# A DLRM tower on one core: 13 instead of 7 embedding tables looked up by one-hot matmuls, Gram matmuls behind the last gather

## The chip, the cores and the metric

The kernel runs on 1 core of a Trainium2 chip. The core has five engines with queues of their own: PE (matmul), DVE (VectorE), ACT (ScalarE), POOL (GpSimd) and SP (SyncE, which here only issues transfers), and 16 DMA engines that they share. The metric is device microseconds per execution; the lower the better. The traces come from separate, profiled executions.

## The reference

A batch of 512 rows. Each row has a dense vector of 128 numbers and 26 ids, one for each embedding table. One table has 125,000 rows, nine have 12,500, eight have 1,250 and eight have 1,000; a table row is 128 fp32 numbers.

```python
e = jnp.stack([tbl_0[ids[:, 0]], ..., tbl_25[ids[:, 25]]], axis=1)       # 512 x 26 x 128
combined = jnp.concatenate([dense_features[:, None, :], e], axis=1)      # 512 x 27 x 128
interactions = jnp.einsum('bnd,bmd->bnm', combined, combined)            # 27 x 27 Gram matrix of each row
z = jnp.concatenate([dense_features, interactions[:, TRIU_I, TRIU_J]], axis=1)
h = jnp.concatenate([z, dense_features], axis=1)                         # 128 + 351 + 128 columns
h = jnp.maximum(h @ W_top1 + b_top1, 0.0)                                # 512
h = jnp.maximum(h @ W_top2 + b_top2, 0.0)                                # 256
y = h @ W_top3                                                           # 1
```

## The kernel before

The batch is worked in four **tiles** of 128 rows. A feature vector gets to the place where the Gram matmuls read it, `vecs_t` (number d on partition d, then tile, row, slot), in one of two ways.

**Gathered tables** (the 19 largest). POOL issues one indirect transfer for each tile and table (L273), 76 in all, in order of tiles; each brings 128 table rows to `vecs`, which has room for two tiles. PE turns them by transposes, four slots at a time (`turn`, L329, groups of slots in `GROUPS`, five to a tile with the dense vector in slot 0), into one of two PSUM tiles `turned`, and DVE copies them to `vecs_t` (`copy_slots`, L422). POOL may write a group of tile t + 2 once the turn of the same group of tile t is done.

**Looked-up tables** (seven with 1,000 rows). SP loads the whole table (L231, L234) and the ids, repeated on all partitions (L236). The table lies in 7 blocks of 128 rows and one of 104. ACT rounds it to `table_hi` (L478), DVE forms the rest, `table_lo` (`split_table`, L414). For each block a one-hot matrix, table row by batch row, is made from the ids: six by DVE in one comparison each (`make_one_hot`, L407), two by ACT in two operations each (L491, L497). PE multiplies each block's high and low part with it (`look_up`, L347), all 512 batch rows at once, summing in PSUM, and ACT copies the sum to `vecs_t` (L502).

**Gram and layers**, for each tile. `products` (L366) issues 128 matmuls of 29 x 27, one for each batch row; in the trace each is two records. DVE and ACT copy the blocks to `prods` (`copy_products`, L210 and L215), each half of them. `mlp1` (L285, L287) is the first layer, in four quarters, `mlp2` (L309) the second and `mlp3` (L316) the third; ACT applies bias and relu (L461, L470), and DVE copies the result out of PSUM (L390). The sum of a lookup lies in the PSUM tiles of the Gram, so the first Gram also waits for the last lookup's copy.

Each engine works through its own list in order: `TENSOR_STEPS`, `VECTOR_STEPS`, `SCALAR_STEPS`. A wait at the head of an engine's queue holds all behind it. Before, PE's list puts tile 0's turns between the lookups and then, tile by tile, a Gram, with the next tile's turns and this tile's layers between Grams. SP issues the loads in order and holds a table's load until a buffer of raw table is free.

## Time and profile before

| | us |
|---|---|
| median of 3 timed runs | 135.42 |
| lowest, highest | 133.78, 136.95 |
| span of the profiled execution | 176.1 |
| PE busy, 1520 matmul records | 101.0 |
| DVE busy | 67.0 |
| ACT busy | 61.3 |
| POOL busy, 76 of 84 instructions are gathers | 79.1 |
| mean granted clock of TensorE, share of full speed | 0.806 |

For the profiled execution no other time than its span is given. The page says for how long each engine was busy, in 40 slices, and who released whom; an idle time put down to "issue" is one in which the engine waited for nothing that the profile shows. PEld is the loading of weights, which runs beside PE. Times within an execution count from its first instruction. Matmul records overlap, so the step from one start to the next is the pace, not the duration of one. A gather's record ends when its descriptors are written; its bytes move after that.

### The profile page before, as it was taken

The page shows a single profiled execution, that of the slowest core. Times are in us where ns is not written, and L with a number is a line of the kernel's source. Part 1 is how long each engine was busy: PE and PEld are TensorE (multiplying, and loading weights), DVE is VectorE, ACT ScalarE, POOL GpSimd, SP SyncE. Part 2 cuts the span into 40 slices and gives each one's busy share as a digit, 9 for nine tenths or more (in the row PEclk, how much of TensorE's full clock was granted, in tenths as well). Part 3 has the DMA queues.
Part 4 walks back from the last instruction along what each step waited for, and adds up shares of the span by engine and source line. Part 5 has one row for each costly group of instructions (what it writes and reads, how often), then busy time and mean ns, then how long its engine had stood idle before and what let it go on. Part 6 is the DMA issues. An engine that isn't in the chain of part 4 may idle for free.

```text
span 176.1 us, 3483 instructions
## 1 busy us (share of the span) xinstructions
PE 101.0 (57%) x1520; PEld 87.4 (50%) x1520; DVE 67.0 (38%) x117; ACT 61.3 (35%) x115; POOL 79.1 (45%) x84
## 2 busy tenths in 40 slices
PE   0059977529993211100005579378894989663983
PEld 0048756428872001000005479277893989553972
DVE  3588899524514000000000762008652793246000
ACT  2695997450841000000000820029411760247021
POOL 4777787777777777777720477600000000000000
PEclk9999997987998555555555678858999699998799
DMA  5986666992121212111210021200000000000000
GB/s 132 294 284 212 217 203 190 327 368 79 48 60 45 60 45 60 45 60 45 60 30 4 19 60 45 63 4 0 4 0 4 4 0 4 4 4 0 4 0 0
DMA packets 6773, 13.57 MB, mean 77 GB/s; under 512 B 2253, under 2 KB 3493, under 8 KB 6630
## 3 DMA queue, kind: packets, MB, share of 16 engines
q1 hardware_dynamic: 4325, 8.36, 14.9%
q0 software_dynamic: 2432, 4.99, 9.3%
q8 instruction: 12, 0.20, 0.5%
q14 instruction: 4, 0.02, 0.1%
HBM read 13.34 MB, written 0.00 MB: 76 GB/s over the span
## 4 chain that ended last, share of the span: by engine, by line
PE 36%; issue 31%; POOL 12%; DVE 12%; DMA 6%; ACT 2%; ACTq 0%; DVEq 0%
PE h_ps L287 14%; POOL vecs L273 12%; PE gram L366 10%; DVE prods L210 9%; PE gram L347 5%; DMA vecs<-tbl,idx 5%; PE h_ps L285 3%; PE turned L329 3%; DVE prods L215 1%; ACT vecs_t L502 1%; DVE vecs_t L422 1%; DMA idx<-ids 1%; PE h_ps L309 1%; ACT h L461 1%; PE h_ps L316 0%
## 5 line engine op out<-in xcount | busy, mean ns | idle before, releaser
L273 POOL DMA_INDIRECT vecs<-tbl,idx x76 | 78.2, 1029 | 33.6 <-issue 22.6
L366 PE MATMUL gram<-vecs_t 128*29 128x27 f32 x1024 | 18.0, 209 | 45.6 <-issue 43.9
L210 DVE COPY prods<-gram 29x192 f32<-29x192 f32 x32 | 15.7, 492 | 65.3 <-PE gram L366 64.4
L366 PEld LDWEIGHTS gram<-vecs_t 128*29 128x29 f32 x1024 | 14.6, 125 | 49.5 <-issue 47.4
L210 ACT COPY prods<-gram 29x192 f32<-29x192 f32 x32 | 15.8, 495 | 56.4 <-PE gram L366 55.7
L422 DVE COPY vecs_t<-turned 128x512 f32<-128x512 f32 x20 | 21.3, 1098 | 17.7 <-PE turned L329 14.2
L287 PE MATMUL h_ps<-prods,w_sb 128*128 128x128 f32 x192 | 26.5, 292 | 0.0
L287 PEld LDWEIGHTS h_ps<-prods,w_sb 128*128 128x128 f32 x192 | 25.1, 208 | 0.1
L347 PE MATMUL gram<-one_hot,table_hi 128*128 128x512 f32 (+1 forms) x56 | 25.1, 447 | 0.0
L347 PE MATMUL gram<-one_hot,table_lo 128*128 128x512 f32 (+1 forms) x56 | 24.3, 435 | 0.0
L407 DVE TENSOR_SCALAR one_hot<-ids_all,row_of 128x512 fp32r<-128x512 int32 x42 | 17.3, 482 | 5.5 <-PE gram L347 5.5
L329 PE MATMUL turned<-ident,vecs 128*128 128x128 f32 x76 | 14.5, 331 | 7.5 <-DMA vecs<-tbl,idx 7.0
L329 PEld LDWEIGHTS turned<-ident,vecs 128*128 128x128 f32 x76 | 11.5, 174 | 9.3 <-DMA vecs<-tbl,idx 7.9
L461 ACT ACTIVATE h<-h_ps,small_sb 128x128 f32<-128x128 f32 x16 | 4.6, 369 | 31.0 <-PE h_ps L287 17.4
L347 PEld LDWEIGHTS gram<-one_hot,table_hi 128*128 128x128 f32 (+1 forms) x56 | 12.3, 219 | 2.7
L347 PEld LDWEIGHTS gram<-one_hot,table_lo 128*128 128x128 f32 (+1 forms) x56 | 12.2, 217 | 2.7
L502 ACT COPY vecs_t<-gram 128x512 f32<-128x512 f32 x7 | 7.9, 1130 | 13.5 <-PE gram L347 11.0
L285 PE MATMUL h_ps<-dense_t,w_dense 128*128 128x128 f32 x32 | 7.2, 310 | 7.8 <-DVE prods L215 4.7
L414 DVE TENSOR_TENSOR table_lo<-table,table_hi 128x1024 fp32r<-128x1024 f32 x7 | 8.6, 1225 | 5.0 <-ACT table_hi L478 4.3
L285 PEld LDWEIGHTS h_ps<-dense_t,w_dense 128*128 128x128 f32 x32 | 5.5, 214 | 8.8 <-DVE prods L215 5.3
L491 ACT ACTIVATE distance<-ids_all,row_of 128x512 f32<-128x512 int32 x14 | 9.3, 710 | 0.5 <-DMA ids_all<-ids_t 0.5
L497 ACT ACTIVATE one_hot<-distance,one 128x512 fp32r<-128x512 f32 x14 | 9.2, 708 | 0.0
(26 smaller groups left out, 47.4 us busy)
## 6 DMA issues: line engine op xcount, KB each, us to landing
table<-tbl SPq DMA_DIRECT2D x7, 448.0 KB
w_sb<-w SPq DMA_DIRECT2D x1, 2048.0 KB
ids_all<-ids_t SPq DMA_DIRECT2D x7, 256.0 KB, 5.1
vecs<-tbl,idx POOLq DMA_INDIRECT x76
w_sb<-w SPq DMA_DIRECT2D x1, 512.0 KB
table<-tbl SPq DMA_DIRECT2D x7, 52.0 KB
dense_rows<-dense SPq DMA_DIRECT2D x1, 256.0 KB, 5.2
idx<-ids SPq DMA_DIRECT2D x1, 52.0 KB, 2.1
```

The lines of the kernel that those rows point to most:

```text
L210: copy(prods[QUAD * k:QUAD * k + ROWS, t % 2, :, q::QUADS], src[0:ROWS, :, FIRST_SLOT[k]:FIRST_SLOT[k] + CHUNKS] .rearrange("p b c -> p c ...
L273: nc.gpsimd.indirect_dma_start(out=vecs[:, t % 2, s, :], out_offset=None, in_=tables[f], in_offset=bass.IndirectOffsetOnAxis(ap=idx[:, t, ...
L285: nc.tensor.matmul(h1_ps[:, o, :], w_dense[:, cols], dense_t[:, t, :], start=True, stop=False)
L287: mm = nc.tensor.matmul(h1_ps[:, o, :], w1_sb[:, 2 + c, cols], prods[:, t % 2, c, :], start=False, stop=(c == CHUNKS - 1))
L329: mm = nc.tensor.transpose(turned[k % 2][:, j, :], vecs[:, t % 2, s, :] if s else dense_rows[:, t, :], ident[:])
L347: mm = nc.tensor.matmul(looked_up[j % 2], part[0:rows, j % PARTS, c, :], one_hot[0:rows, j % 2, c, :], start=(c == 0 and part is table_hi) ...
L366: mm = nc.tensor.matmul(gram[t % 2][QUAD * q:QUAD * q + ROWS, blk, 0:N], x[:, 0:ROWS], x[:, 0:N], start=True, stop=True)
L407: nc.vector.tensor_scalar(one_hot[:, j % 2, c, :], ids_all[:, j, :], at, None, ALU.is_equal).then_inc(hot_ok, 1)
L422: nc.vector.tensor_copy(vecs_t[:, t, :, slots[0]:slots[-1] + 1].rearrange("d r s -> d s r"), turned[k % 2][:, 0:len(slots), :]).then_inc(s ...
L491: nc.scalar.activation(distance[:, i, :], ids_all[:, j, :], ACT.Square, bias=at, scale=-1.0).then_inc(distance_ok, 1)
L497: nc.scalar.activation(one_hot[:, j % 2, c, :], distance[:, i, :], ACT.Relu, bias=one[:], scale=-1.0).then_inc(hot_scalar, 1)
L502: nc.scalar.copy(vecs_t[:, :, :, TURNED + j], looked_up[j % 2].rearrange("p (t r) -> p t r", t=TILES)).then_inc(look_out, 1)
```

## The change

Thirteen tables are looked up (all eight with 1,000 rows, five with 1,250) and 13 gathered, in 52 transfers. A looked-up table now lies on 125 partitions in 8 or 10 equal blocks (`TP`, `NBLK`), 114 in all, loaded in two parts of 112 and 13 partitions. DVE makes all one-hot blocks, into a ring of 16 (`HOT`) whose places come free one by one; ACT makes none, and does the slot copies of the first 13 turns in DVE's place. A lookup does all its high matmuls, then all its low ones; it has four places for its sums instead of two, and there are three buffers for raw tables. The ids come in three loads, and the weights behind table 7. The layouts of ids and dense vectors in memory are changed so that each partition reads one piece.

In the step lists, a lookup and a turn alternate 13 times, then come the other three turns (there are sixteen now, four to a tile), and then the four Grams with the layers between them.

```diff
-LOOKED_UP = 7
+LOOKED_UP = 13
+TP = 125
+SPREAD = 112
...
+NBLK = [TABLE_ROWS[f] // TP for f in LOOKUPS]
...
+RAW = 3
+PARTS = 2
+HOT = 16
+SUMS = 4
...
-TENSOR_STEPS = (
-    FIRST_STEPS + [("products", 0, 0)] + turns(1, EARLY, EARLY + 2) + first_layer(0)[:1]
-    + turns(1, EARLY + 2, NG) + first_layer(0)[1:]
...
+KEEP = 2
+IDS_PARTS = [(0, 1), (1, 4), (4, LOOKED_UP)]
+WEIGHTS_AFTER = 7
+LOOK_TURNS = [(step, n) for n in range(LOOKED_UP) for step in ("look", "turn")]
+TENSOR_STEPS = LOOK_TURNS + [("turn", n) for n in range(LOOKED_UP, len(TURNS))] + [
+    ("products", 0), ("products", 1),
+    ("layer1", 0), ("products", 2), ("layer2", 0), ("layer1", 1), ("layer3", 0), ("products", 3), ("layer2", 1),
+    ("layer1", 2), ("layer3", 1), ("layer2", 2), ("layer1", 3), ("layer3", 2), ("layer2", 3), ("layer3", 3),
+]
+VECTOR_STEPS = [("weights", 0)] + [("turn", n) for n in range(LOOKED_UP, len(TURNS))] + [
+    ("products", 0), ("products", 1), ("products", 2), ("layer3", 0), ("products", 3), ("layer3", 1),
+    ("layer3", 2), ("layer3", 3),
 ]
...
+            load_ids(0)
+            sp.dma_start(dense_rows[:], dense).then_inc(dense_in, 16)
+            load_table(sp, 1)
+            load_ids(1)
+            load_table(sp, 2)
+            load_ids(2)
+            for j in range(3, LOOKED_UP):
+                load_table(sp, j)
+                if j == WEIGHTS_AFTER:
+                    sp.dma_start(w1_sb[:], w1).then_inc(w_in, 16)
...
             def look_up(j):
-                if j >= 2:
-                    pe.wait_ge(look_out, j - 1)
+                if j >= SUMS:
+                    pe.wait_ge(look_out, j - SUMS + 1)
+                pe.wait_ge(hi_ok, j + 1)
+                for c in range(NBLK[j]):
+                    k = FIRST_HOT[j] + c
+                    pe.wait_ge(hot_ok, k + 1)
+                    nc.tensor.matmul(looked_up[j % SUMS], table_hi[0:TP, j % PARTS, c, :], one_hot[0:TP, k % HOT, :],
+                                     start=(c == 0), stop=False)
                 pe.wait_ge(lo_ok, j + 1)
...
-                mm.then_inc(look_ok, 1)
+                for c in range(NBLK[j]):
+                    k = FIRST_HOT[j] + c
+                    nc.tensor.matmul(looked_up[j % SUMS], table_lo[0:TP, j % PARTS, c, :], one_hot[0:TP, k % HOT, :],
+                                     start=False, stop=(c == NBLK[j] - 1)).then_inc(hot_used, 1)
             def products(t):
-                pe.wait_ge(slots_out, NG * (t + 1))
+                turn_is_out(pe, min(NG * (t + 1), LOOKED_UP) - 1)
+                turn_is_out(pe, NG * (t + 1) - 1)
                 pe.wait_ge(extra_out, 2 * (t + 1))
                 if t == 0:
                     pe.wait_ge(look_out, LOOKED_UP)
...
+            def make_one_hot(j):
+                if j == 0:
+                    dve.wait_ge(rows_ok, len(SIZES))
+                for i, (a, b) in enumerate(IDS_PARTS):
+                    if j == a:
+                        dve.wait_ge(ids_in[i], 16)
+                for c in range(NBLK[j]):
+                    k = FIRST_HOT[j] + c
+                    if k >= HOT:
+                        dve.wait_ge(hot_used, k - HOT + 1)
+                    at = row_of[0:TP, SIZES.index(NBLK[j]), c:c + 1]
+                    nc.vector.tensor_scalar(one_hot[0:TP, k % HOT, :], ids_all[0:TP, j, :], at, None,
+                                            ALU.is_equal).then_inc(hot_ok, 1)
...
+            for j in range(LOOKED_UP):
+                make_one_hot(j)
                 split_table(j)
...
+            load_table(act, 0)
+            for j in range(PARTS):
                 table_hi_part(j)
...
-                if j + 2 < LOOKED_UP:
-                    make_one_hot_blocks(j + 2)
-                if j + 3 < LOOKED_UP:
-                    table_hi_part(j + 3)
+                if j + PARTS < LOOKED_UP:
+                    table_hi_part(j + PARTS)
+                copy_slots(act, nc.scalar.copy, slots_act, j)
+                if j % NG == 0:
+                    extra_copies(j // NG)
```

PE's queue, before, behind the last lookup (`turned` is a turn, `gram<-vecs_t` a Gram, `h_ps` a layer; `gathered1_2` is tile 1's group 2):

```order
L329 MATMUL turned<-ident,dense_rows 128x128 [waits slots_out,gathered1_0]
L329 MATMUL turned<-ident,vecs 128x128 x3
L329 MATMUL turned<-ident,vecs 128x128 [waits slots_out,gathered1_1]
L329 MATMUL turned<-ident,vecs 128x128 x3
L366 MATMUL gram<-vecs_t 29x27 [waits look_out,extra_out,slots_out]
L366 MATMUL gram<-vecs_t 29x27 x127
L329 MATMUL turned<-ident,vecs 128x128 [waits slots_out,gathered1_2]
L329 MATMUL turned<-ident,vecs 128x128 x3
L329 MATMUL turned<-ident,vecs 128x128 [waits slots_out,gathered1_3]
L329 MATMUL turned<-ident,vecs 128x128 x3
L285 MATMUL h_ps<-dense_t,w_dense 128x128 [waits w_in,w_dense_ok,prods_act,prods_dve]
```

PE's queue, changed, from turn 13 (tile 3's group 1) on:

```order
L311 MATMUL turned<-ident,vecs 128x128 [waits slots_act,gathered3_1]
L311 MATMUL turned<-ident,vecs 128x128 x3
L311 MATMUL turned<-ident,vecs 128x128 [waits slots_act,gathered3_2]
L311 MATMUL turned<-ident,vecs 128x128 x3
L311 MATMUL turned<-ident,vecs 128x128 [waits slots_dve,gathered3_3]
L311 MATMUL turned<-ident,vecs 128x128
L344 MATMUL gram<-vecs_t 29x27 [waits extra_out,look_out,slots_act]
L344 MATMUL gram<-vecs_t 29x27 x127
L344 MATMUL gram<-vecs_t 29x27 [waits extra_out,slots_act]
L344 MATMUL gram<-vecs_t 29x27 x127
L279 MATMUL h_ps<-dense_t,w_dense 128x128 [waits w_in,w_dense_ok,prods_act,prods_dve]
```

Tile 0's Gram stood behind tile 1's second turn, and each further Gram behind its own tile's turns; now all four stand behind the last turn of tile 3. The turns of tiles 1 to 3 that lay between Grams and layers lie between lookups.

DVE's queue, before, for the first two looked-up tables (`table_lo` is a split, `vecs_t<-turned` the copy of a turn):

```order
L414 TENSOR_TENSOR table_lo<-table,table_hi 128x1024 [waits hi_ok]
L407 TENSOR_SCALAR one_hot<-ids_all,row_of 128x512 [waits ids_all_in0,rows_ok]
L407 TENSOR_SCALAR one_hot<-ids_all,row_of 128x512 x5
L414 TENSOR_TENSOR table_lo<-table,table_hi 128x1024 [waits hi_ok]
L407 TENSOR_SCALAR one_hot<-ids_all,row_of 128x512 [waits ids_all_in1]
L407 TENSOR_SCALAR one_hot<-ids_all,row_of 128x512 x5
L422 COPY vecs_t<-turned 128x4x128 [waits turned_ok]
L414 TENSOR_TENSOR table_lo<-table,table_hi 128x1024 [waits hi_ok]
```

DVE's queue, changed, for the first tables (split and one-hots of tables 0, 1, 2 and on):

```order
L382 TENSOR_SCALAR one_hot<-ids_all,row_of 125x512 [waits ids_in0,rows_ok]
L382 TENSOR_SCALAR one_hot<-ids_all,row_of 125x512 x7
L389 TENSOR_TENSOR table_lo<-table,table_hi 125x1024 [waits hi_ok]
L382 TENSOR_SCALAR one_hot<-ids_all,row_of 125x512 [waits ids_in1]
L382 TENSOR_SCALAR one_hot<-ids_all,row_of 125x512 x7
L389 TENSOR_TENSOR table_lo<-table,table_hi 125x1024 [waits hi_ok]
L382 TENSOR_SCALAR one_hot<-ids_all,row_of 125x512 [waits hot_used] x8
L389 TENSOR_TENSOR table_lo<-table,table_hi 125x1024 [waits hot_used,hi_ok]
```

The turn's copy is gone from between the tables, one-hots go ahead of their table's split, eight of them where there were six, and from the third table on each waits for a place in the ring (`hot_used`).

## Rows read from the trace of the kernel before

**Rows 1.** Waits: engine, line, what was waited for: total us, times, longest us.

```profile
PE gram L366 <- issue: 43.9, 33, 2.6
```

**Rows 2.** Timeline (start us, us, engine, what, [idle before]), PE, tile 0's Gram matmuls.

```profile
52.93 0.45 PE L366 MATMUL gram<-vecs_t 128*29 128x27 f32 x34 [0.39 <-ACT vecs_t L502]
...
87.83 0.20 PE L366 MATMUL gram<-vecs_t 128*29 128x27 f32 x1 [2.60 <-issue]
...
94.82 2.61 PE L366 MATMUL gram<-vecs_t 128*29 128x27 f32 x187 [0.50 <-issue]
```

**Rows 3.** Stretches: length, busy us (records) of PE, PEld, DVE, ACT, POOL; clock; DMA.

```profile
52.90:97.50 44.60, 8.71 (x257) 6.42 (x258) 1.80 (x3) 0.84 (x3) 27.54 (x29) 0.53 0.15 45
...
111.20:119.10 7.90, 4.28 (x257) 3.70 (x258) 0.01 (x1) 1.15 (x5) 1.89 (x2) 0.65 0.11 29
...
137.60:156.50 18.90, 15.28 (x353) 14.44 (x353) 10.00 (x16) 7.23 (x18) 0.00 (x0) 0.91 0.01 3
```

**Rows 4.** Timeline of PE, the Gram matmuls of tiles 2 and 3.

```profile
133.00 1.55 PE L366 MATMUL gram<-vecs_t 128*29 128x27 f32 x161 [0.64 <-DVE vecs_t L422]
...
136.57 1.00 PE L366 MATMUL gram<-vecs_t 128*29 128x27 f32 x95 [2.03 <-issue]
...
151.57 1.78 PE L366 MATMUL gram<-vecs_t 128*29 128x27 f32 x189 [0.64 <-DVE vecs_t L422]
...
155.73 0.77 PE L366 MATMUL gram<-vecs_t 128*29 128x27 f32 x67 [2.38 <-issue]
```

**Rows 5.** DMA queues of the whole span: packets, MB, share of 16 engines.

```profile
q8 instruction: 12, 0.20, 0.5%
```

**Rows 6.** Timeline of POOL, gathers 1, 19, 40, 64 and 76.

```profile
3.12 1.10 POOL L273 DMA_INDIRECT vecs<-tbl,idx  x1 [1.46 <-DMA idx<-ids]
...
29.81 0.94 POOL L273 DMA_INDIRECT vecs<-tbl,idx  x1 [0.30 <-issue]
...
58.31 0.94 POOL L273 DMA_INDIRECT vecs<-tbl,idx  x1 [0.30 <-issue]
...
88.27 0.94 POOL L273 DMA_INDIRECT vecs<-tbl,idx  x1 [0.30 <-issue]
...
112.48 0.94 POOL L273 DMA_INDIRECT vecs<-tbl,idx  x1 [0.30 <-issue]
```

**Rows 7.** DMA view, 112 to 115 us: bytes moved in 40 slices of 0.075 us.

```profile
GB/s 0 219 0 0 0 0 0 0 0 0 0 218 164 273 164 55 0 0 0 0 0 0 0 0 0 0 0 0 328 218 219 109 0 0 0 0 0 0 0 0
```

**Rows 8.** Timeline of DVE, one looked-up table: its split and six one-hot blocks.

```profile
21.35 1.23 DVE L414 TENSOR_TENSOR table_lo<-table,table_hi 128x1024 fp32r<-128x1024 f32 x1 [0.72 <-issue]
...
22.49 2.46 DVE L407 TENSOR_SCALAR one_hot<-ids_all,row_of 128x512 fp32r<-128x512 int32 x6
```

**Rows 9.** Timeline of PE, lookup matmuls after a wait and in the last stretch.

```profile
30.39 0.63 PE L347 MATMUL gram<-one_hot,table_hi 128*128 128x512 f32 x1
...
30.82 0.63 PE L347 MATMUL gram<-one_hot,table_lo 128*128 128x512 f32 x1
...
48.28 0.40 PE L347 MATMUL gram<-one_hot,table_hi 128*128 128x512 f32 x1
...
48.52 0.39 PE L347 MATMUL gram<-one_hot,table_lo 128*128 128x512 f32 x1
```

**Rows 10.** Timeline of PE, first-layer quarter, turn behind it, tile 3's last turn.

```profile
129.67 0.39 PE L285 MATMUL h_ps<-dense_t,w_dense 128*128 128x128 f32 x2
...
131.24 0.60 PE L329 MATMUL turned<-ident,vecs 128*128 128x128 f32 x4
...
149.80 0.60 PE L329 MATMUL turned<-ident,vecs 128*128 128x128 f32 x4
```

**Rows 11.** Timeline of DVE, half of the copies of tile 2's Gram blocks.

```profile
137.62 2.08 DVE L210 COPY prods<-gram 29x192 f32<-29x192 f32 x4 [4.57 <-PE gram L366]
...
139.73 0.33 DVE L215 COPY prods<-gram 27x96 f32<-27x96 f32 x1
```

**Rows 12.** Timeline of PE, what follows the last first layer.

```profile
169.45 0.60 PE L316 MATMUL h_ps<-h,small_sb 128*1 128x128 f32 x4
```

More of the change, by code:

```diff
@@ L51 @@
 TURNED = 1 + len(GATHERED)
-FULL = [TABLE_ROWS[f] // P for f in LOOKUPS]
-LAST = [TABLE_ROWS[f] % P for f in LOOKUPS]
-MAX_BLOCKS = max(FULL) + 1
-PARTS = 3
-BY_SCALAR = 2
-SIZES = sorted(set(FULL))
+NBLK = [TABLE_ROWS[f] // TP for f in LOOKUPS]
+MAX_BLOCKS = max(NBLK)
+SIZES = sorted(set(NBLK))
+RAW = 3
+PARTS = 2
+HOT = 16
+SUMS = 4
+FIRST_HOT = [sum(NBLK[:j]) for j in range(LOOKED_UP)]
+assert all(TABLE_ROWS[f] % TP == 0 for f in LOOKUPS)
 PER_GROUP = 4
@@ L62 @@
 NG = len(GROUPS)
+TURNS = [(t, g) for t in range(TILES) for g in range(NG)]
 QUARTERS = H1 // P
-def turns(t, first, end):
-    return [("turn", t, g) for g in range(first, end)]
-def first_layer(t):
-    return [("layer1", t, q) for q in range(QUARTERS)]
-EARLY = 2
-FIRST_TURNS = turns(0, 0, NG) + turns(1, 0, EARLY)
-FIRST_LOOKS = [("look", j, 0) for j in range(LOOKED_UP)]
-FIRST_STEPS = [x for pair in zip(FIRST_TURNS[:NG], FIRST_LOOKS) for x in pair]
-FIRST_STEPS += FIRST_LOOKS[NG:] + FIRST_TURNS[NG:]
@@ L120, in product_rows, with dlrm_tower @@
     return where
-def dlrm_tower(nc, dense, ids, ids_t, tables, w1, w2, small, out):
+def dlrm_tower(nc, dense, idx_rows, ids_look, tables, w1, w2, small, out):
     with ExitStack() as ctx:
@@ L177, in dlrm_tower @@
         hot_ok = sem("hot_ok")
[L178 removed]
+        hot_used = sem("hot_used")
         look_out = sem("look_out")
[L180 removed]
+        gathered = [[sem(f"gathered{t}_{g}") for g in range(NG)] for t in range(TILES)]
         ident_zero = sem("ident_zero")
@@ L199, in dlrm_tower, with looked, turn_is_out, load_table @@
         BY_ENGINE = 2 * (QUADS + 1)
+        def looked(j):
+            return FIRST_HOT[j] + NBLK[j]
+        def turn_is_out(engine, n):
+            if n < LOOKED_UP:
+                engine.wait_ge(slots_act, n + 1)
+            else:
+                engine.wait_ge(slots_dve, n + 1 - LOOKED_UP)
+        def load_table(engine, j):
+            f = LOOKUPS[j]
+            rows = tables[f].rearrange("(p c) d -> p c d", p=TP)
+            if j >= RAW:
+                engine.wait_ge(lo_ok, j - RAW + 1)
+            for a, b in [(0, SPREAD), (SPREAD, TP)]:
+                engine.dma_start(table[a:b, j % RAW, 0:NBLK[j], :], rows[a:b]).then_inc(table_in[j % RAW], 16)
+        def copy_slots(engine, copy, done, n):
+            t, g = TURNS[n]
+            engine.wait_ge(turned_ok, n + 1)
+            slots = GROUPS[g]
+            copy(vecs_t[:, t, :, slots[0]:slots[-1] + 1].rearrange("d r s -> d s r"),
+                 turned[n % 2][:, 0:len(slots), :]).then_inc(done, 1)
         def copy_products(engine, copy, done, t, quads):
@@ L568 @@
     out = nc.dram_tensor("y", (B, 1), F32, kind="ExternalOutput").ap()
-    dlrm_tower(nc, dense, ids, ids_t, tables, w1, w2, small, out)
+    dlrm_tower(nc, dense, idx_rows, ids_look, tables, w1, w2, small, out)
     r = run_bass_kernel_spmd(nc, [arrays], core_ids=[0])
```

269 lines of the change are left out of this document (87 added, 182 removed).

## The prediction

> **What bounds the kernel now.** I read the spans first: the profiled execution spans 176.1 us, the timed runs 133.8 to 137.0 us. A trace 40 us longer than the runs must hold time that they do not have, so the next view was the waits: PE's Gram matmuls (L366) stand idle 43.9 us in 33 gaps with nothing that releases them [rows 1]. The timeline puts nearly all in tile 0's Gram: from 52.9 to 94.8 us single matmuls lie up to 2.6 us apart while POOL issues gathers, and once POOL stops, 187 records follow in 2.6 us [rows 2, 6]. I read these gaps as the profile's own. As a stretch, tile 0's Gram took 44.6 us and tile 1's 7.9 [rows 3]; tiles 2 and 3, with no gathers beside them, took 133.00 to 137.57 and 151.57 to 156.50, 4.7 us on average, with one gap of 2.0 to 2.4 us in each [rows 4]. With 4.7 in place of 44.6 and 7.9 the span is 176.1 - 39.9 - 3.2 = **133.0 us**. The median run, 135.4, is 2.4 above; that I take as what lies around the span, and put on again at the end.
>
> In those 133 us: until 52.9 PE alternates turns and lookups; then it goes through four tiles, about 19 us each (137.6 to 156.5 [rows 3]), and gathers for tiles 2 and 3 arrive under that work. POOL's stream would then end at 88.27 + 12 x 1.248 = 103.2 at the last issue, 105.1 with the transfer, just ahead of tile 3's last turn (149.8 - 43.1 = 106.7 [rows 10]). So the kernel is bound by PE with its copies, and the gathers are hidden, barely.
>
> **The change, part by part.**
>
> *Gathers.* 52 instead of 76. Quiet, one follows another every (88.27 - 58.31) / 24 = 1.248 us. In the first 19, while DVE makes one-hots and splits, it is (29.81 - 3.12) / 18 = 1.483 [rows 6]. DVE's five sets of such work in that stretch are 5 x 3.6 = 18.0 us of 26.7, 67% [rows 8]. The change keeps DVE at it without turn copies, some 97%: the extra 0.235 us grows to 0.34, a pitch of 1.59.
>
> *Lookups on DVE.* One block takes 2.46 / 6 = 0.41 us, a split of 8 blocks 1.14 [rows 8], one of 10 by size 1.43. Eight tables of 8 blocks at 4.42 and five of 10 at 5.53 give 63.0 us (ScalarE makes no blocks now). From about 6 us, when ids and the first table are in, DVE ends at 69.
>
> *Lookups on PE.* 228 matmuls at 0.23 us at the high clock, 52 us; after a wait they go at 0.43 [rows 9]. Per table 3.7 (4.6) and a turn of 0.6: under DVE's 4.42 (5.53), hence hidden, if the clock holds. It then trails DVE by one table's low half: lookups end near 72 to 76.
>
> *Last gather.* By 69 us POOL is 41.4 pitches on; the other 9.6 go at 1.248: issue at 69 + 12.0 = 81.0, done 0.94 later, transfer 1.0 later (gather 76 ended at 113.42, its bytes moved until 114.4 [rows 6, 7]). **T0 = 83 us.** The bounds: at 1.248 throughout the last gather lands at 68.7 and the lookups with three turns decide, 74.5; at the worst of the lookups (below) 90.
>
> *What waits for T0.* The step list puts turns 13, 14 and 15 ahead of Gram 0; turn 15 waits for the last gather, and everything behind it on PE's queue with it: all four Grams and all twelve layer steps. DVE's queue holds the three turn copies ahead of its product copies, ScalarE's queue waits on Gram 0. Nothing of tiles 0 to 2 runs under the gathers any more.
>
> *The tail from T0.* A turn of four tables to the next Gram took 131.24 to 133.00, 1.76 [rows 4, 10]; two tables, 1.2. Four Grams at 4.7: 18.8. A first layer is four quarters of 1.57 (129.67 to 131.24) [rows 10], 6.3, times four 25.2. A second layer has 16 records where a quarter has 14: 1.8, three times 5.4 (the fourth is in the end). Two third layers 1.0. From the last first layer to the end 176.1 - 169.45 = 6.65 [rows 12]. The product copies take 2 x 2.45 = 4.9 us [rows 11]: Gram 1 hides tile 0's but for 0.2, later ones lie under the first layers. Second layer 2 waits for its relus, 1.3. The clock will be low after the waits for the last gathers: the mean of the stretch with the 187 records is 0.53, mostly the 1.2 GHz level [rows 3], and they took 13.9 ns each where tile 2's 161 took 9.6 [rows 2, 4]; for the first Gram and what follows it, 1.3. Sum 1.2 + 18.8 + 25.2 + 5.4 + 1.0 + 6.65 + 1.5 + 1.3 = **61.1 us**. By 83 + 61 = 144.1 the change costs 11.1 us on 133.0, for 24 gathers fewer.
>
> *Loads.* Tables and ids bring 7.3 + 3.4 MB in place of 3.5 + 1.8; the weights go out behind table 7. I cost this at nothing: DVE is two blocks of work ahead through the ring of 16, and T0 is some 7 us behind the lookups. If that cover goes, it is the second rival.
>
> *The single gap in each Gram.* Rows show one gap of 2.03 and 2.38 us in tiles 2 and 3 after 161 and 189 records, with 95 + 96 + 189 = 380 matmul records between them (257 of the 353 from 137.6 to 156.5 are the Gram's [rows 3]), each with its load, about 760 instructions, and instruction transfers of 0.20 MB / 12 = 17 KB [rows 4, 5]. I count the gap in each Gram, in both kernels. The Trainium skill (Runtime: NRT & Kernel Launch, Instruction fetch mechanics) says that engines fetch 16 KiB blocks of 256 instructions and that crossing a block is mostly hidden. The trace agrees on the size and speaks against the hiding; by the rule both kernels lose their gaps, which is the third rival.
>
> **The rivals.**
>
> 1. *The Gram gaps are real waits of PE beside the gathers* (faster). Place: tile 0's and tile 1's Gram, 43.1 us over plain in the trace. In the changed kernel no gather runs beside a Gram, so whatever of this is real in the timed runs comes back. It decides from 11.1 + 2.7 = 13.8 us on. With 16 real the time is 135.4 + 11.1 - 16 = 130.5. For it: the gaps stop within a few us of POOL's pause [rows 2, 6]. Against: 133.0 + 16 would be 149, 14 over what was timed. 0.08.
>
> 2. *The lookups outlast the gathers.* PE's clock falls in the waits for one-hot blocks and for gathers; a table at 0.43 us per matmul takes 7 to 8.6 us where DVE takes 4.4 to 5.5, and then one-hots wait for free slots of the ring, and table loads for splits. The trace has three such slow starts, each some eight matmuls long [rows 9]. At 1.3 to 1.6 us each over most of the 13 tables the lookups end near 87, T0 is 90: 153.5. 0.15.
>
> 3. *The gap in the Grams is hidden in unprofiled runs.* Gram 2.5 us. The changed kernel saves 6.6 (2.4 of 8.8 turn into waits for tile 0's copies): 137.5. Before, the last gather at 105.2 would then decide: 105.2 + (176.1 - 149.8) - 2.2 = 129.3, counted from tile 3's last turn [rows 10]. Difference 8.2: 143.6. 0.13.
>
> 4. *The one-hots don't slow the gathers* (125 partitions, another order). T0 = 74.5, time 138. Against: gathers of 1.1 to 2.0 us lie only beside DVE's lookup work. 0.10.
>
> 5. *The gathers stand still during DVE's lookup work.* Then the last lands at 3.1 + 63.0 + 63.6 + 1.9 = 131.6 and the time is 195. Against: the trace has 19 gathers going through with DVE 67% busy, at 0.235 us extra each. 0.02. The Trainium skill (SBUF — State Buffer, SBUF: two separate sides) states the rule behind this: DVE's two-port operations lock GpSimd out of the shared ports for the whole instruction, so that it cannot write descriptors. The trace agrees that there is a loss, not that it is whole.
>
> That the change doesn't do what it says is excluded by the order: four Grams behind sixteen turns.
>
> **How the numbers follow.** The forecast has 0.52: 144.1 + 2.4 = **146.5 us**; its own range, from the pitch (1.48 to 1.65) and the low clock, is 142 to 151. The range for 8 in 10 is **137 to 155**: it takes in rivals 2, 3 and most of 4, and leaves out 1, 5 and the edges. Two per cent is about what a measurement can tell here: 132.7 to 138.1. Faster: rival 1, 0.08. Within: the half of rival 4, a little of 3 and of the forecast, 0.12. Slower: 0.80.
>
> **What would show it.** In the changed profile: the waits list loses the 40 us of gaps, so its span lies near 144 and only some 2 to 3 us under the timed run, whereas before it lay 40 over. POOL: 52 gathers, pitch 1.5 to 1.6 until DVE's last split (about 69), 1.25 behind it. PE: Gram 0 starts at 84, waiting for the last gather and its copy; Gram 0 and 1 end near 93.5, and from there PE is over 85% busy. DVE: no long wait in the lookups. I am wrong if Gram 0 starts under 78 or over 88; if Gram 0 and 1 together take far from 9.4, because two bursts behind one another may drain what was fetched ahead; if PE's lookups run at 0.43 for more than a third of them; or if span and timed run again lie far apart, since then what I took off the profile of before was not the profile's own.

## The result, and the profile after

The changed kernel took **168.25 us** (median of 4 runs, 165.08 to 171.39), the kernel before, beside it, 135.56 (133.78 to 136.95): 1.246 times as long, interval 1.2204 to 1.2716. I had 146.5, range 137 to 155. The direction was right, the size was 22 us short. The profiled execution spans 169.3 us and its timed run is 171.39, so span and run lie 2.1 apart. It is the longest of the four runs, two of which (165.08 and 166.78) are 5 to 6 us faster, so the trace shows a little more loss than the median.

The lines of the page on POOL's gathers and DVE's one-hots (busy us, mean ns | idle before):

```profile
L249 POOL DMA_INDIRECT vecs<-tbl,idx x52 | 80.5, 1547 | 19.5 <-issue 15.2
L382 DVE TENSOR_SCALAR one_hot<-ids_all,row_of 125x512 fp32r<-125x512 int32 x114 | 46.6, 479 | 19.4 <-PE gram L328 14.3
```

52 gathers keep POOL busy for 80.5 us, as long as 76 did. The timeline of POOL shows which ones were long; against the first and the last gather of [rows 6] stand 5.58 and 100.64:

```profile
5.58 1.10 POOL L249 DMA_INDIRECT vecs<-tbl,idx  x1 [3.90 <-DMA idx<-idx_rows]
...
15.66 4.00 POOL L249 DMA_INDIRECT vecs<-tbl,idx  x1 [0.30 <-issue]
...
37.32 4.79 POOL L249 DMA_INDIRECT vecs<-tbl,idx  x1 [0.30 <-issue]
...
64.91 1.28 POOL L249 DMA_INDIRECT vecs<-tbl,idx  x1 [0.30 <-issue]
66.49 1.28 POOL L249 DMA_INDIRECT vecs<-tbl,idx  x1 [0.30 <-issue]
68.08 5.06 POOL L249 DMA_INDIRECT vecs<-tbl,idx  x1 [0.30 <-issue]
73.44 5.06 POOL L249 DMA_INDIRECT vecs<-tbl,idx  x1 [0.30 <-PE turned L311]
78.81 5.06 POOL L249 DMA_INDIRECT vecs<-tbl,idx  x1 [0.30 <-issue]
...
100.64 0.95 POOL L249 DMA_INDIRECT vecs<-tbl,idx  x1 [0.31 <-issue]
```

DVE's timeline of the same stretch answers to [rows 8]:

```profile
63.61 4.04 DVE L382 TENSOR_SCALAR one_hot<-ids_all,row_of 125x512 fp32r<-125x512 int32 x10
67.58 1.47 DVE L389 TENSOR_TENSOR table_lo<-table,table_hi 125x1280 fp32r<-125x1280 f32 x1
68.98 4.04 DVE L382 TENSOR_SCALAR one_hot<-ids_all,row_of 125x512 fp32r<-125x512 int32 x10
72.94 1.47 DVE L389 TENSOR_TENSOR table_lo<-table,table_hi 125x1280 fp32r<-125x1280 f32 x1
```

The gather at 68.08 begins in the split and ends at 73.14, just behind the end of the ten one-hots (73.02). The one at 37.32 ends at 42.11; a run of eight one-hots (38.74, 3.25 us) ended at 41.99. All five gathers of 4 us and more end 0.12 to 0.14 us behind the end of a run of eight or ten one-hots, also where the next split follows at once. These five stood until the run was over. There are 13 such runs, and not every one holds a gather: beside the ten one-hots from 63.61 to 67.65, just as unbroken, two gathers took 1.28 us each. What decides which gather is caught is not shown. PE, whose list puts a turn behind each lookup, waits with it (waits: total us, times, longest):

```profile
PE turned L311 <- DMA vecs<-tbl,idx: 24.3, 7, 8.6
...
DVE one_hot L382 <- PE gram L328: 14.3, 3, 9.4
```

and DVE in its turn finds no free place for one-hots. PE's timeline from the last turns on, against [rows 2, 4, 10]:

```profile
100.72 1.11 PE L311 MATMUL turned<-ident,vecs 128*128 128x128 f32 x4 [4.35 <-DMA vecs<-tbl,idx]
103.30 0.69 PE L311 MATMUL turned<-ident,vecs 128*128 128x128 f32 x2 [1.46 <-DMA vecs<-tbl,idx]
103.91 2.51 PE L344 MATMUL gram<-vecs_t 128*29 128x27 f32 x180
108.38 1.82 PE L344 MATMUL gram<-vecs_t 128*29 128x27 f32 x128 [1.95 <-issue]
111.71 1.82 PE L344 MATMUL gram<-vecs_t 128*29 128x27 f32 x128 [1.51 <-issue]
115.16 1.21 PE L344 MATMUL gram<-vecs_t 128*29 128x27 f32 x76 [1.63 <-issue]
...
128.52 3.26 PE L292 MATMUL h_ps<-h,w_sb 128*128 128x128 f32 x16
...
154.38 2.05 PE L292 MATMUL h_ps<-h,w_sb 128*128 128x128 f32 x16 [0.77 <-ACT h L420]
```

Gram 0 starts at 103.91. Two Grams behind one another have three gaps, the last two 128 records apart. Behind Gram 2 a second layer takes 3.26 us, a later one 2.05. The stretches from Gram 0 on (columns as in [rows 3]):

```profile
103.90:116.40 12.50, 7.40 (x514) 6.95 (x513) 5.25 (x11) 4.61 (x10) 0.00 (x0) 0.50 0.02 6
...
123.97:128.60 4.63, 2.56 (x258) 2.42 (x257) 0.00 (x0) 1.14 (x4) 0.00 (x0) 1.00 0.01 4
128.60:138.60 10.00, 10.00 (x74) 9.83 (x75) 4.60 (x10) 5.36 (x13) 0.00 (x0) 0.83 0.01 2
```

Grams 0 and 1 ran at a mean clock of 0.50, the 1.2 GHz level. In tile 0's first layer the clock rose (mean 0.83 from 116.4 to 123.9), Gram 2 ran at 1.00, and in the second layer behind it (129.5 to 131.6) it was at 0.50 again.

### The profile page after: what moved, and what is told of

The parts are those of the page before. It is cut to its first block, busy times and chain, and to the rows that moved or that the text cites. A ratio compares the mean times of both kernels' runs of the same rounds, so it can differ in the third digit from the quotient of the medians.

```text
span 169.3 us, 3712 instructions
## 1 busy us (share of the span) xinstructions
PE 123.7 (73%) x1612; PEld 106.0 (63%) x1612; DVE 86.5 (51%) x176; ACT 70.4 (42%) x112; POOL 81.3 (48%) x60
## 4 chain that ended last, share of the span: by engine, by line
POOL 46%; PE 30%; issue 15%; DMA 4%; ACT 2%; POOLq 1%; ACTq 0%; DVE 0%
POOL vecs L249 46%; PE h_ps L281 13%; PE gram L344 7%; PE h_ps L292 6%; DMA idx<-idx_rows 3%; PE h_ps L279 3%; DMA vecs<-tbl,idx 2%; ACT h L420 1%; POOLq L98 1%; PE h_ps L299 1%; PE turned L311 0%; ACT h L429 0%; DVE y_sb L368 0%; ACTq L98 0%; ACTq L418 0%
## 5 line engine op out<-in xcount | busy, mean ns | idle before, releaser
L249 POOL DMA_INDIRECT vecs<-tbl,idx x52 | 80.5, 1547 | 19.5 <-issue 15.2
L382 DVE TENSOR_SCALAR one_hot<-ids_all,row_of 125x512 fp32r<-125x512 int32 x114 | 46.6, 479 | 19.4 <-PE gram L328 14.3
L323 PE MATMUL gram<-one_hot,table_hi 125*128 125x512 f32 x114 | 36.9, 479 | 7.9 <-DMA dense_rows<-dense 7.9
L323 PEld LDWEIGHTS gram<-one_hot,table_hi 125*128 125x128 f32 x114 | 25.5, 234 | 13.1 <-issue 7.9
L328 PE MATMUL gram<-one_hot,table_lo 125*128 125x512 f32 x114 | 30.9, 419 | 0.0
L328 PEld LDWEIGHTS gram<-one_hot,table_lo 125*128 125x128 f32 x114 | 23.9, 210 | 5.9 <-DVE table_lo L389 0.3
L311 PEld LDWEIGHTS turned<-ident,vecs 128*128 128x128 f32 x52 | 7.0, 160 | 25.4 <-DMA vecs<-tbl,idx 24.3
L195 ACT COPY vecs_t<-turned 128x512 f32<-128x512 f32 (+1 forms) x13 | 13.8, 1062 | 13.1 <-PE turned L311 13.1
L389 DVE TENSOR_TENSOR table_lo<-table,table_hi 125x1024 fp32r<-125x1024 f32 (+1 forms) x13 | 17.1, 1319 | 1.0 <-ACT table_hi L437 1.0
L437 ACT CAST table_hi<-table 125x1024 fp32r<-125x1024 f32 (+1 forms) x13 | 15.2, 1169 | 5.3 <-DMA table<-tbl 5.3
L292 PE MATMUL h_ps<-h,w_sb 128*128 128x128 f32 x64 | 10.7, 335 | 1.5 <-ACT h L420 1.5
L292 PEld LDWEIGHTS h_ps<-h,w_sb 128*128 128x128 f32 x64 | 9.8, 242 | 2.2 <-ACT h L420 2.1
```

What stands on the lines that cost most here:

```text
L249: nc.gpsimd.indirect_dma_start(out=vecs[:, t % KEEP, s - 1, :], out_offset=None, in_=tables[f], in_offset=bass.IndirectOffsetOnAxis(ap=idx ...
L292: mm = nc.tensor.matmul(h2_ps[:, o, :], w2_sb[:, c, o * P:(o + 1) * P], h1[:, t % 2, c, :], start=(c == 0), stop=(c == H1 // P - 1))
L311: mm = nc.tensor.transpose(turned[n % 2][:, i, :], vecs[:, t % KEEP, s - 1, :] if s else dense_rows[:, t, :], ident[:])
L323: nc.tensor.matmul(looked_up[j % SUMS], table_hi[0:TP, j % PARTS, c, :], one_hot[0:TP, k % HOT, :], start=(c == 0), stop=False)
L328: nc.tensor.matmul(looked_up[j % SUMS], table_lo[0:TP, j % PARTS, c, :], one_hot[0:TP, k % HOT, :], start=False, stop=(c == NBLK[j] - 1)). ...
L382: nc.vector.tensor_scalar(one_hot[0:TP, k % HOT, :], ids_all[0:TP, j, :], at, None, ALU.is_equal).then_inc(hot_ok, 1)
```

## The experiments

All kernels of a comparison ran on one chip with runs of the kernel before between them. **That kernel's median was 135 to 137 us on chips 3, 7 and 15 and in the first comparison, and 179.6 and 179.68 on chip 1.** Times are compared only within a chip; where only the ratio can be carried over, it is given.

### What holds the gathers up

*few_hot*: only the first 16 one-hot blocks are made, the other 98 comparisons are left out, so its result is not that of the reference.

```diff
-                    pe.wait_ge(hot_ok, k + 1)
+                    pe.wait_ge(hot_ok, min(k + 1, HOT))
...
-                        dve.wait_ge(hot_used, k - HOT + 1)
+                        continue
```

> The changed kernel with only the first 16 one-hot blocks made (the other 98 are left out and the first 16 used again); splits, lookups, turns and gathers stay. Theory A (gathers are held up by DVE's runs of one-hots): no gather over 2.2 us, pitch under 1.35 us, last gather issued near 72 us instead of 100.6, Gram 0 starts near 76 instead of 103.9, time near 141 us. Rival (gathers are held up by transfers or by the splits): gathers of 4 to 5 us stay, Gram 0 after 95, time over 158 us.

*one_port*: each one-hot in an accumulating form, slower on DVE.

```diff
+        hits = sb("hits", [P, HOT])
...
-                    nc.vector.tensor_scalar(one_hot[0:TP, k % HOT, :], ids_all[0:TP, j, :], at, None,
-                                            ALU.is_equal).then_inc(hot_ok, 1)
+                    nc.vector.tensor_scalar(one_hot[0:TP, k % HOT, :], ids_all[0:TP, j, :], at, 0.0,
+                                            ALU.is_equal, ALU.add,
+                                            accum_out=hits[0:TP, k % HOT:k % HOT + 1]).then_inc(hot_ok, 1)
```

> The changed kernel with each one-hot written by the form that also sums its result, which I expect to run one element per cycle: 0.6 us a block instead of 0.40, 114 x 0.2 = 23 us more on DVE. Theory A (only fast one-hots, which take both of DVE's port pairs, hold up gathers): no gather over 2.5 us, pitch near 1.3, last gather issued near 73 us; DVE's lookup work then decides, ends near 93 to 96, Gram 0 near 98, time 160 to 164 us. Rival (any busy DVE holds them up): gathers of 4 us and more stay and Gram 0 starts after 108, time over 172 us.

Both ran on chip 1: few_hot 171.3 us (0.95 of before there, 0.9384 to 0.9617), one_port 190.08 (1.0418, 1.0247 to 1.0589). The changed kernel's 52 gathers took 73.2 us on that chip (after_again), few_hot's 57.1 and one_port's 53.4; 38 and 44 of the 52 took 0.94 or 0.95 us, at a pitch of 1.25. In one_port that was so although DVE was busy with one-hots for 77.1 us. So it isn't DVE's load as such that holds gathers up. Two things differ in one_port, though: the form is slower, and behind each one-hot its trace has a second instruction of 81 ns, DVE_READ_ACCUMULATOR, 114 in all, so the runs are broken there too; it can't tell these apart. A few gathers were still held: one_port's longest took 1.93 us, beside a split, and one of few_hot 3.45, across the last of its one-hots and two splits behind one another. Both predicted times were missed. Neither became faster than the changed kernel (161.95 on that chip); why is in the part on chip 1.

*breaks*: the changed kernel with 114 one-element memsets, on chip 15.

```diff
+        tiny = sb("tiny", [P, 128])
...
                                             ALU.is_equal).then_inc(hot_ok, 1)
+                    nc.vector.memset(tiny[:, k:k + 1], 0.0)
```

> The changed kernel with a memset of one element on VectorE after each one-hot block (114 of them, some 60 ns each, so 7 us more work there). Theory A (a gather stands still for a whole run of two-port one-hots because no gap between them lets it in; the longest were 5.06 us): no gather is longer than 2.5 us, the last one is issued up to 8 us earlier than in the changed kernel (93.3 in its run beside these), time 153 to 162 us. Rival B (it is the sum of the one-hots' time that counts, not that they are unbroken): gathers are as long as before or longer, last gather issued at 93 to 100, time 161 to 170 us (161.95 without the memsets).

*after_third*: the changed kernel again, on chip 7.

> The changed kernel, unchanged, beside its variants. Theory A (its time hardly depends on the chip, since its PE waits for gathers and one-hots and has its Grams after the gathers): 160 to 169 us whatever the kernel before takes; gathers held up for 4 to 5 us at least twice. Rival B (it shifts as the kernel before does): under 150 us beside a before of 136 us.

breaks took **150.42 us** (147.55 to 151.43), 1.1133 of before (1.0638 to 1.1627); after_third 163.34 (162.17 to 165.51), 1.192 (1.1809 to 1.2031). The gathers of breaks in its page, its last one and its first Gram:

```profile
L250 POOL DMA_INDIRECT vecs<-tbl,idx x52 | 60.4, 1161 | 19.2 <-issue 15.2
...
80.28 0.95 POOL L250 DMA_INDIRECT vecs<-tbl,idx  x1 [0.30 <-issue]
...
83.33 2.18 PE L345 MATMUL gram<-vecs_t 128*29 128x27 f32 x180
```

after_third's last gather is at 93.60, its longest took 5.06 us (the only one over 4 us, where at least two were expected); in breaks none takes over 2.2 us, the 114 memsets cost DVE 6.7 us, and DVE no longer waits for PE's lookups. Gathers took 20.1 us less than in the first trace, and Gram 0 starts 20.6 us earlier (13.5 before after_third's 96.84). The one-hots are the same and DVE's work is longer; only the runs are broken. The same comparison can be made on chip 15 alone, where gram_early_again (below) ran with unbroken one-hots:

```profile
L251 POOL DMA_INDIRECT vecs<-tbl,idx x52 | 74.5, 1433 | 19.4 <-issue 15.2
...
94.61 0.94 POOL L251 DMA_INDIRECT vecs<-tbl,idx  x1 [0.30 <-issue]
```

Its gathers took 14.1 us more than those of breaks and the last was issued 14.3 us later; two took 4.80 and 5.06 us. So it is shown that breaking the runs frees the gathers, and the time fell below theory A's range. That a gather stands for a whole run is true of some only: gram_early, with the same unbroken runs on chip 1, had none over 2.87 us, and its gathers still took 72.3 us. With the runs broken a gather of breaks took 1161 ns on average, one of one_port 1028. How the memset lets a gather in was not tried.

### What the place of the Grams costs

*gram_early*: Gram 0 right behind the last lookup, the last turns behind it.

```diff
-TENSOR_STEPS = LOOK_TURNS + [("turn", n) for n in range(LOOKED_UP, len(TURNS))] + [
-    ("products", 0), ("products", 1),
-    ("layer1", 0), ("products", 2), ("layer2", 0), ("layer1", 1), ("layer3", 0), ("products", 3), ("layer2", 1),
+TENSOR_STEPS = LOOK_TURNS + [
+    ("products", 0), ("turn", 13), ("products", 1),
+    ("layer1", 0), ("turn", 14), ("products", 2), ("turn", 15),
+    ("layer2", 0), ("layer1", 1), ("layer3", 0), ("products", 3), ("layer2", 1),
...
```

> The changed kernel with Gram 0 directly behind the last lookup and turns 13, 14 and 15 between Grams 0, 1, 2 and the layers, in PE's list and DVE's. Theory A (the step order costs the wait for the last gather only): Gram 0 starts near 94 instead of 103.9, and the time falls by 7 to 10 us, to 159. Rival (a Gram beside gathers has the gaps seen before): what is won is lost in gaps in Gram 0 or 1 of some us or more, time 165 to 180.

*gram_early_again*: the same file on chip 15.

> The changed kernel with tile 0's Gram right behind the lookups and the last three turns behind it, without memsets, beside a kernel before that is expected at 135 to 138 us. Theory A (where gathers do not hold up PE, the early Gram fills the 3 to 10 us in which PE otherwise waits for the last gathers): 153 to 160 us, a ratio of 1.12 to 1.17 where the changed kernel had 1.192 and 1.246. Rival B (the last lookups end as late as the last gathers, so there is nothing to fill): 161 to 168 us.

*early_breaks*: this order and the memsets, on chip 3.

> The changed kernel with 13 tables, one-element memsets after the one-hots, and tile 0's Gram right behind the lookups, the last turns behind it. Theory A (in the version with the memsets alone, 150.42 us, the last gathers and the lookups end together at 80 to 83, so there is nothing left for the early Gram to fill): 147 to 152 us. Rival B (the early Gram is worth what it was without memsets beside a slow kernel before, 2.7 us, or more): 143 to 147 us.

gram_early took 159.25 us on chip 1 (0.8832, 0.8715 to 0.895). That is theory A's time, but not its gain of 7 to 10 us, since the changed kernel takes 161.95 there; and its Gram 0, from 83.64 on, had the rival's gaps until 95.13. gram_early_again took **153.17** (150.53 to 155.56; 1.1087, 1.0934 to 1.1239), and early_breaks 150.01 (1.1128, 1.0904 to 1.1352). So the order alone brings a ratio of 1.192 to 1.109, the memsets alone to 1.113, both together again to 1.113: they are two cures for one wait. The order lets PE do Gram 0 (87.33 in gram_early_again) while the late gathers, the last at 94.61, come in. What neither touches is the last lookup: Gram 0 cannot start before it ends, at 78 to 86, and 64 us follow Gram 0's start (147.7 - 83.33 in breaks).

### How many tables

*breaks7*: the kernel before with the memsets. *nine_tables*, *ten_tables*: the same with more tables, two buffers of split tables instead of three and a ring of 8 for the ids. (*breaks10*, ten tables with the three buffers, gave no time: it does not fit in SBUF, where `one_hot` needs 40,960 bytes and 36,160 are left.)

```diff
-LOOKED_UP = 7
+LOOKED_UP = 10
...
-PARTS = 3
+PARTS = 2
```

> The kernel before (7 tables) with a one-element memset on VectorE after each of its 42 one-hot blocks. Theory A (unbroken runs of one-hots hold a gather up until the run is over): its first 40 gathers, which came at a pitch of 1.43 us, come at 1.27 to 1.35, so all end 3 to 6 us earlier, and the time is 130 to 134 us beside 136 (or 174 to 182 where the kernel before takes 180). Rival B: the memsets only lengthen VectorE's work by 2.5 us and the time stays within 1% of the kernel before or is 1 to 2 us more.

> The same with 9 tables (68 gathers). Theory A: last gather issued at 92 to 100, time 124 to 133 us where the kernel before takes 137. Rival B: 137 to 146 us.

> The kernel before with 10 tables looked up (64 gathers) in its own order, split tables in 2 buffers instead of 3, ids in a ring of 8, and a one-element memset after each one-hot block on VectorE. Theory A (with broken runs gathers come at 1.25 to 1.4 us, and the balance of gathers against lookups lies between 7 and 13 tables): last gather issued at 88 to 96 (103.3 in the clean profile of the kernel before), tile 0's Gram behind the last lookup at 62 to 68, time 122 to 132 us where the kernel before takes 137. Rival B (the lookups end at 75 or later because each waits for VectorE's and ScalarE's buffers, and the 64 us behind them follow): 138 to 150 us.

breaks7 took 136.1 us beside 137.29 (0.9843, 0.96 to 1.0087: no difference), nine_tables 137.51 beside 135.42 (1.0242, 1.0011 to 1.0472), ten_tables 143.1 (139.5 to 147.13). All three theories A missed in time, and breaks7 in the pitch too: its first 40 gathers came every 1.42 us, as in base_again. The last gathers of the other two and Gram 0 of ten_tables came where they were expected. The first Gram and the last gather of each, in order of their times:

```profile
54.15 3.07 PE L370 MATMUL gram<-vecs_t 128*29 128x27 f32 x204 [0.39 <-ACT vecs_t L509]
103.42 0.94 POOL L277 DMA_INDIRECT vecs<-tbl,idx  x1 [0.30 <-issue]
```

```profile
55.98 2.12 PE L370 MATMUL gram<-vecs_t 128*29 128x27 f32 x169 [0.38 <-ACT vecs_t L509]
96.38 0.94 POOL L277 DMA_INDIRECT vecs<-tbl,idx  x1 [0.30 <-issue]
```

```profile
63.58 2.11 PE L370 MATMUL gram<-vecs_t 128*29 128x27 f32 x150 [0.38 <-ACT vecs_t L509]
91.50 0.94 POOL L277 DMA_INDIRECT vecs<-tbl,idx  x1 [0.31 <-issue]
```

Their spans are 135.4, 135.4 and 145.3 (the last is ten_tables' longest run): behind Gram 0 come 81.3, 79.4 and 81.7 us, whether the last gather is issued at 103 or at 91. In this order the work behind the last lookup is the bound, gathers are not, and in these three spans what pushes Gram 0 back is paid in full. In breaks7 gather 19 began where it had (30.26 against 30.13 in base_again): six one-hots in a row held up too little to matter. On chips 3, 7 and 15 no version beat the kernel before.

*old13*, the kernel before with 13 tables in its own order, ran on chip 1 and took 160.24, 161.92, 186.54 and 191.68 us.

> The kernel before with 13 tables looked up and nothing else of the change (two buffers of table parts instead of three, eight places for ids). The lookups last longer (13 x 4.6 + 11, to 75 us), Gram 0 stands behind them and behind tile 1's second turn only. Theory A (the number of tables costs little, the step order and the run of fast one-hots the rest): Gram 0 starts near 76 to 80, gathers are over by 80, no long gaps, 150 to 158 us. Rival (13 lookups are themselves the cost): Gram 0 after 90 and over 165 us.

That is no ratio to build on; it only shows that there, too, 13 tables could be under 179.7, and that neither theory had the time.

### The chip on which the kernel before takes 180 us

*base_look* is the kernel before on chip 1, *base_again* on chip 7, *after_again* the changed kernel on chip 1.

> The kernel before, unchanged, profiled a second time. Theory A (the 40 us of gaps in tile 0's Gram belong to the profiled execution): the timed value stays near 135 us, and the gaps come again with about the same size, or shrink, in the profile alone. Theory B (the gaps are real waits of PE beside the gathers that come and go from execution to execution): the time of this execution lies near 178 us when its span lies near 176.

> The kernel before, unchanged, for one profile beside the next three. The run of it beside the kernels with spaced gathers was timed at 136.15 us, the runs beside the earlier ones at 179.6. Theory A (whether gathers that go out one behind the other hold up PE's instructions differs from chip to chip): where the timed runs are near 136 us, this profile has a span of 131 to 135 us, no gaps of 10 us or more inside tile 0's Gram, and no waits named remote over 5 us on VectorE or ScalarE; where they are near 180, span 177 to 180 and such waits of 20 us and more. Rival B (it is the profiling of an execution that makes the gaps): the span is 176 us or more while the timed runs are near 136.

> The changed kernel, unchanged, on the same chip as the others. In the last comparison the kernel before took 179.6 us where it had taken 135.4 earlier, and the gaps beside its gathers were in its timed executions too. Theory A (the gaps are real, they come and go with the chip or the hour, and the changed kernel has few of them since its gathers are done before the Grams): 165 to 171 us as before, whatever the kernel before takes. Rival (the whole chip was slower): above 185 us if the kernel before takes 180.

Waits of base_look (span 177.9, timed 179.66; "remote" is another engine's report):

```profile
ACT vecs_t L502 <- remote: 37.7, 3, 23.8
DVE vecs_t L422 <- remote: 37.5, 1, 37.5
...
PE gram L366 <- DVE vecs_t L422: 30.3, 3, 29.0
```

Grams of tiles 0 and 2 and the last gather in base_again (span 136.0, timed 137.88):

```profile
55.41 2.85 PE L366 MATMUL gram<-vecs_t 128*29 128x27 f32 x204 [0.39 <-ACT vecs_t L502]
59.53 0.64 PE L366 MATMUL gram<-vecs_t 128*29 128x27 f32 x52 [1.28 <-issue]
...
91.98 2.37 PE L366 MATMUL gram<-vecs_t 128*29 128x27 f32 x161 [0.63 <-DVE vecs_t L422]
95.82 1.18 PE L366 MATMUL gram<-vecs_t 128*29 128x27 f32 x95 [1.47 <-issue]
...
103.28 0.94 POOL L273 DMA_INDIRECT vecs<-tbl,idx  x1 [0.30 <-issue]
```

Span and timed run lie 1.8 to 1.9 apart on both chips. On chip 7 the gaps of [rows 1, 2] are absent, though gathers go out at the same pitch beside the Gram. On chip 1 they are real and part of the timed run. after_again took 161.95 us there, under both theories' times, 0.8964 of before (0.8882 to 0.9046): the same change that costs 19 to 25% on other chips gains 10% on this one, presumably (this is argued, not shown) because it puts little of PE's work beside the quick gathers.

On chip 1 I took gathers that follow each other every 1.25 us to be what holds PE up, wherever it is in its list. few_hot and one_port, with few held-up gathers, had PE stand beside them: in one_port from 43.5 to 49.1 one lookup matmul every 2.8 us; in few_hot, by its waits:

```profile
PEld gram L323 <- issue: 26.3, 3, 12.4
...
ACT vecs_t L441 <- remote: 23.2, 3, 14.2
```

The pitch alone does not decide it: in few_hot gathers went out every 1.25 us from 31 us on, and PE's lookups beside them ran with one gap of 0.87 us until about 47.

*gated7* holds POOL back until Gram 0 and Gram 1 are done; *gated13* is gram_early with the last ten gathers held until Gram 1 is done and Grams 0 to 2 ahead of the last turns.

```diff
+                    if (t, g) in ((2, 0), (2, 3)):
+                        pool.wait_ge(gram_ok, 1 if g == 0 else 2)
```

> The kernel before with two waits more on POOL: tile 2's gathers start when Gram 0 is done, those of its group 3 when Gram 1 is done. Theory A (PE is held up while gathers go out one behind another): tile 0's Gram takes about 5 us instead of 10 to 44, tile 1's about 5, and the time is 136 to 145 us where the kernel before takes 180 beside it. Rival (the gaps have nothing to do with POOL): Gram 0 as long as before, and 3 to 5 us more in all, 183.

> The changed kernel with Grams 0, 1 and 2 ahead of the last three turns, and with POOL holding its last ten gathers back until Gram 1 is done. Theory A: Gram 0 starts at 83 to 94 without gaps beside gathers, Gram 0 and 1 take 12 us, the rest as before: 148 to 157 us, some 3 to 8 below the version with early Grams and free gathers (159). Rival (the ten gathers, 12.5 us, now come late for Gram 3 or hold up the layers beside them): 160 us or more.

gated7 took 171.78 us, 0.9533 (0.9428 to 0.9639), not theory A's 136 to 145: its Gram 0 was freed (61.62 to 66.75) and, once POOL went on, a first layer stood instead (DVE's remote wait 42.7 us). gated13 took 161.06, the rival's time, and no better than gram_early. *spaced7* and *spaced13* put memsets on POOL between gathers.

```diff
+                                pool.wait_ge(paused, pauses[0])
+                                nc.gpsimd.memset(pause[:], 0.0).then_inc(paused, 1)
```

> The kernel before (7 tables) with one memset of a [128, 384] tile on POOL after each gather from the last group of tile 1 on, nothing else changed. Theory A (unhindered gathers hold up PE): PE's transposes of the turns and its reports reach ScalarE and VectorE within a few us instead of up to 37.5 us late, and although POOL's last gather ends some 15 us later than in the kernel before, the time falls from 179.7 to 150 to 165 us. Rival B (the late reports have nothing to do with the pitch of the gathers): the waits named remote on ScalarE and VectorE stay at 20 us or more, and the time is 180 to 195 us.

> The changed kernel with the first Gram right behind the lookups, and after each gather of tile 3 two memsets of a [128, 384] tile on POOL, so that those gathers no longer go out one right behind the other. Theory A (gathers that go out at a pitch of 1.25 us beside nothing else hold up PE's instructions and the reports of PE's semaphores): the gathers of tile 3 come at a pitch of 2 us or more, tile 0's Gram, which stood with gaps for 11.5 us of its 13.9 in the kernel without the memsets, runs through in about 6, so layers come earlier, and the time is 148 to 156 us (159.25 without the memsets), though the last gather ends later. Rival B (PE is held up by POOL's work or by its own fetches, however the gathers are spaced): the gaps stay or grow with the longer stretch of gathers, 160 to 170 us.

They came to chip 15, where nothing holds PE up, and so could not test this: spaced7 146.97 us beside 136.15 (1.0981, 1.0708 to 1.1255), its last gather 12 us later at 115.3; spaced13 157.02, its last gather at 102.1. That spaced gathers would free PE on chip 1 stays open, and so does what is different in that chip. spaced7 shows only that on the others the gathers are hidden by little.

## Why the prediction was wrong

1. **The time of before, rebuilt.** 133.0 us and a last gather at 103.2 in the place of 176.1 and 112.48: base_again has 136.0 and 103.28, with one gap in each of the Grams shown. The reduction was right for kernels timed near 136 us. The reason I gave was not: on chip 1 the gaps are no product of the profile. So the profile of before was presumably taken on chip 1 or one like it and the runs elsewhere; on which chips is not known. Rival 1 rested on the same row, and on chip 1 its direction, faster, is the result.

2. **The pitch of the gathers: the step that failed.** I took 1.59 us near DVE and 1.25 behind it. Near DVE it was (86.88 - 5.58) / 40 = 2.03, behind it 1.25 as said. From 5.58 to 100.64 it is 95.06 / 51 = 1.86 us on average, 17.2 us more than the 77.9 that I had from first to last. (In the two other traces of the changed kernel the average is 1.72 and 1.73 and the last gather at 93.34 and 93.60, so some 7 us of the miss come and go.) The first gather came 2.5 us later than in [rows 6] (the ids landed late; I had costed the new loads at nothing), the last transfer took 0.7 longer. Sum 20.3; the last gather landed at 103.3 instead of 83. I had scaled the loss by DVE's busy share, from rows in which at most six one-hots stand in a row [rows 8]. The loss depends on whether they go unbroken: breaks does the same one-hots in more of DVE's time at (76.53 - 5.33) / 48 = 1.48 near DVE, which is the lower end of my own range. So the rule that I gave 0.02 (DVE's two-port operations lock POOL out for the instruction; the Trainium skill, SBUF — State Buffer, SBUF: two separate sides) holds for a part of the gathers: 9 of the 52 took 1.9 us or more, and the five longest ended with the run, not with an instruction of it.

3. **DVE's lookup work.** 63.0 us predicted, 46.6 + 17.1 = 63.7 measured for one-hots and splits. It ended at 85.1 and not at 69: 14.3 us of waits for PE, which I had at zero; of the 5.1 for ids, 4.4 lie ahead of the first one-hot at 6.84, which I had at about 6. The waits for PE follow from step 2: PE waited 24.3 us for gathers, 16.6 of them between lookups, and in breaks, with gathers on time, DVE never waits for PE.

4. **The lookups on PE** ended at 93.3, not 72 to 76, by the same wait; in breaks at 78. Rival 2 had this end, by slow starts after waits. They came too (ten matmuls from 85.85 took 4.62 us at a clock of 0.50, where those from 77.87 took 2.54), but after waits for late gathers; from 58.99 to 82.7 the lookups ran at the high clock. (In rival 3, 8.8 - 2.4 is 6.4 and not 6.6, which changes nothing.)

5. **What waits for T0.** From the last landing to Gram 0 0.6 us (1.2 predicted), and all four Grams and layers behind it, as said.

6. **The tail.** 65.4 us from Gram 0 where I had 61.1 - 1.2 = 59.9. The mis-sized term is the clock, which I had at 1.3 us. Grams 0 and 1 took 12.5 instead of 9.4, which I had named as a sign of error: their 512 records took 7.4 us at a clock of 0.50, 14.4 ns each where tile 2's took 9.6 in [rows 4], 2.4 us more; their three gaps took 5.1 us where I had two of 2.2, 0.7 more. Behind them tile 0's first layer took 7.7 us instead of 6.3 (its first quarter 2.9 instead of 1.57), tile 1's 6.8, and two of the three second layers over 3 us where I had 1.8. The clock did not stay low in between: it was at 1.00 in Gram 2 and at 0.50 again behind that Gram's gap of 2.07 us. In breaks a second layer behind a gap of 1.89 us took 2.05, so why it fell here is open. As for the gaps, two Grams behind one another had three, after 180, 128 and 128 records, but Gram 2 ran 250 records without one and Gram 3 172: they don't come once in 128 records everywhere. That two bursts use up what was fetched ahead, as the prediction feared, would fit this, but no run tests it. Grams 2 and 3 took 4.6 and 5.0, near the 4.7 predicted.

7. **Span and run.** Close together, 2.1 apart, as predicted for the changed kernel.

83 + 20.3 for the last gather, 0.6 to Gram 0, 65.4 of tail and 2.1 around the span are 171.4, the profiled run. The median is 168.25.

## What to carry to other kernels

When a vector engine's fast elementwise work shares the chip with indirect gathers, do not scale the loss by its busy share: look for the longest unbroken run that the change will make. One gather can lose as much as the whole run, though in the first trace only five of 13 runs kept one until their end; in all, the 52 gathers took 72 to 81 us in the traces of the changed kernel and its early Grams, and 60 with broken runs. A one-element instruction between the one-hots brought the kernel from 1.192 to 1.113 of the kernel before, about 11 us. Before fewer gathers are worth anything, ask what follows the last lookup: some 80 us in the old order, 64 in the new, and Gram 0 moved from 55 to 83 in breaks. And when a span and the timed runs lie far apart, do not call the difference the profile's own before the same file has been profiled where it is timed.
